# Selective-scan kernel: the products with B issued behind the first scan of an index, and both products of the next chunk's first two indices inside the last index

## The chip, the cores and the metric

The kernel runs on one core of a Trainium2 chip. The metric is the device time of one execution in microseconds, the median of the runs. Engines are named as in the profile: PE is TensorE, DVE is VectorE, ACT is ScalarE, POOL is GpSimd, SP is SyncE (here it only issues DMAs).

## The reference

The whole program is a block of three layers over x with shape (4, 2048, 256): half of an attention and mixture-of-experts layer, a bidirectional selective scan (Mamba) layer, and again half of the first. Only the selective scan is touched. Cut down, for one direction, with 512 inner channels d and 16 states n:

```python
x  = silu(depthwise_conv4(x) + conv_b)                   # (B, 512, L)
dt, Bm, Cm = split(x_proj_w @ x)                          # 16 + 16 + 16 rows
dt = softplus(dt_w @ dt + dt_b)
def step(h, (dt_t, B_t, C_t, u_t)):                       # over the L tokens
    h = exp(dt_t * A) * h + (dt_t * u_t) * B_t            # h is (B, 512, 16)
    return h, sum_n h * C_t
y = scan(step) + D * x
```

The other direction runs over the reversed tokens, and the two results are added.

## The kernel before

The scan stage is `mamba_scans`. The 4 x 2048 tokens are cut into chunks of 512 (`CH`), 16 chunks for each direction, so the stage handles M = 32 chunks one after the other. The 512 channels are four tiles m of 128 partitions (`DM` = 4). A chunk has 16 indices n (`DS`), one for each state; a pair (n, m) is a unit, and a chunk has 64 units in the order n outer, m inner. `par` is the chunk's parity.

For one index n the work is this:

- **Decay** (ACT, L1911): exp(dt * A) of a unit into one of two PSUM banks. The decay of unit k waits until the scan of unit k - 2 is done.
- **Product with B** for the whole index, 128 x 2048. For 11 of the 16 indices DVE computes it (`times_b` of the vector block, L1969): `du` times a row of B that PE has spread over a PSUM bank (`BANK_B`) with four transposes (`row_b`, L1752). The two buffers `db` alternate. For n in `POOL_N` = (3, 6, 9, 12, 15) POOL computes it from an SBUF row (L1688) into the single buffer `dbp`, three indices ahead: POOL issues the one for n + 3 behind its own work for n.
- **Scan** (DVE, L1998): `tensor_tensor_scan`, one for each unit, 128 x 512, reads the decay, the product and the carried state, and writes `h[n % 4]`.
- **Carry** (ACT, L1871): the last column of `h` is kept for the next chunk. It is issued at the second unit of the next index, when all four scans of index n are done.
- **Times C** (POOL, L1695): `h[n % 4]` times a row of C, 128 x 2048, when the carry is done. POOL's order in a chunk is: times C of 0; product 3; times C of 1, 2, 3; product 6; times C of 4, 5, 6; product 9; times C of 7, 8, 9; product 12; a DMA that adds up softplus; times C of 10, 11; `du` of the next chunk (L1682); times C of 12; product 15; times C of 13, 14, 15.
- **Sum** (PE, L1779): four fp32 matmuls by the identity (eight passes in the trace) add `h * C` up in PSUM. PE does it two indices late (`LAG`). The scan of index n waits (`summed`) for the sum of index n - 4, since `h` has four buffers.

Into the same indices the next chunks' preparation is spread by constants. PE: projection of x at index 0, turning of B at 2, dt projections at 3 to 6, convolution of the chunk after the next at 7 to 14, two halves for each m (`PE_CONV`), and `add_other` at 9 in the second direction. ACT, at the second unit (m = 1): `split` at index 1, `keep_b` at 3, `softplus_in` at 4 to 7, `conv_out` (L1835) at 9, 11, 13 and 15, and `silu` (L1839, L1840: table load, 128 x 2048 activation, table load back) at 15; and at all four units: `read_y` at 2, `softplus_exp` at 8, `softplus_ln` at 9.

PE's row for a DVE product follows the product before: `next_row_b(i, par, n)` stands in PE's index n - 1, waits until DVE has made the product of n, and spreads the row of the next DVE index.

The engines run in the order in which they are written; nothing is reordered. The chunk loop `in_steps` writes 12 of the 32 chunks out (chunks 0 to 3 and 12 to 19) and runs the other 20 in two hardware loops of four chunks for each pass (2 passes over chunks 4 to 11, 3 over chunks 20 to 31). In the loops the semaphore values are computed in registers.

The vector block's order before is, for each index n: at m = 0, if n + 1 (modulo 16) is a DVE index, a wait until every scan issued so far is done (`scanned`), then the product of n + 1, then the four scans of n. So the product of index 0 of the next chunk stands ahead of the scans of index 15, and that of index 1 ahead of the scans of index 0.

Of the kernel before, what the change touches and what calls it, by code (L numbers as in the profile page):

```python
# [20 lines left out]
DI, DS, DTR = 512, 16, 16  # L21
DM = DI // P
# [3 lines left out]
UNITS = DM * DS  # L26
# [4 lines left out]
class Phase:  # L31
# [12 lines left out]
    def sem(self, name):  # L44
        self.sems.append(self.nc.alloc_semaphore(f"{self.tag}_{name}"))
        return self.sems[-1]
# [1456 lines left out]
def mamba_scans(nc, tag, psum, ident, xp, y, both, weights, B, S):  # L1503
# [9 lines left out]
    POOL_N = (3, 6, 9, 12, 15)  # L1513
# [5 lines left out]
    BANK_A, BANK_B, BANK_X = 4, 6, 7  # L1519
    FREE = (BANK_A, BANK_A + 1, BANK_X, 0)  # L1520
    PE_X, PE_TURN, PE_DT, PE_CONV, PE_Y, SP_Y = 0, 2, 3, 7, 9, 11
    A_SPLIT, A_TURN, A_SOFT, A_EXP, A_LN, A_SILU = 1, 3, 4, 8, 9, 15
    G_ADD, G_DU = 9, 11
    EXP_LN = "natural_log_exp_and_others"

    def b_count(i, n):

        made = POOL_N if n in POOL_N else DVE_N
        return len(made) * i + sum(z <= n for z in made)
# [6 lines left out]
    with Phase(nc, tag) as ph:  # L1536
# [34 lines left out]
        scanned, carried, hc_ready, summed = sem("scanned"), sem("carried"), sem("hc_ready"), sem("summed")  # L1571
# [25 lines left out]
        def chunk_of(i, par, n):  # L1597

            return (i, par, n) if n < DS else (i + 1, 1 - par, n - DS)

        with nc.Block() as block:
# [226 lines left out]
            def _(act):  # L1828
# [13 lines left out]
                def split(i):  # L1842
                    act.wait_ge(xp_ps, i + 1)
                    act.wait_ge(bc_out, 16 * i)
                    nc.scalar.activation(xd[:, :], psum[0:BC + DTR, BANK_X, :], ACT.Copy).then_inc(xd_sb, 1)
# [15 lines left out]
                def softplus_exp(i, m):  # L1861
                    act.wait_ge(dt_read, 2 * (DM * i + m + 1))
                    nc.scalar.activation(sp1[:, m, :], sp1[:, m, :], ACT.Exp, scale=-1.0).then_inc(exps, 1)

                def softplus_ln(i, m):
                    act.wait_ge(exps, DM * i + m + 1)
                    nc.scalar.activation(sp1[:, m, :], sp1[:, m, :], ACT.Ln, bias=1.0).then_inc(logs, 1)

                def carry(n, ends, rev):
                    kept = zeros[:, :] if ends else h[n % NH][:, :, LAST[rev]]  # L1870
                    nc.scalar.activation(state[:, n, :], kept, ACT.Copy).then_inc(carried, 1)  # L1871

                def read_y(i, m):
                    act.wait_ge(y_done, DM * i + m + 1)
                    if m == 0:
                        act.wait_ge(stored, 16 * i)
                    nc.scalar.activation(yo[:, m, :], psum[:, m, :], ACT.Copy).then_inc(y_read, 1)
# [22 lines left out]
                def step(i, par, first, opens, ends, way):  # L1900
                    for k, (n, m) in enumerate(UNIT):
                        if k >= 2 or not first:
                            act.wait_ge(scanned, UNITS * i + k - 1)
                        if k == 0 and first:
                            act.wait_ge(dt_ready, 1)
                        elif k == 0:
                            act.wait_ge(dt_added, 16 * i)
                        if m == 1 and (n or not first):
                            act.wait_ge(scanned, UNITS * i + DM * n)
                            carry((n - 1) % DS, ends if n else opens, way(0 if n else -1))  # L1910
                        nc.scalar.activation(psum[:, BANK_A + k % 2, :], dt[par][:, m, :], ACT.Exp, scale=an[way(0)][:, m, n:n + 1]  # L1911
                                             ).then_inc(decay, 1)
                        if n == LAG and not first:
                            read_y(i - 1, m)
                        if n == A_EXP:
                            softplus_exp(i + 1, m)
                        if n == A_LN:
                            softplus_ln(i + 1, m)
                        if m != 1:
                            continue  # L1920
                        if n == A_SPLIT:
                            split(i + 1)
                        if n == A_TURN:
                            keep_b(i + 1, 1 - par)
                        if A_SOFT <= n < A_SOFT + DM:
                            softplus_in(i + 1, 1 - par, n - A_SOFT, way(1))
                        if n > PE_CONV and (n - PE_CONV) % 2 == 0:
                            conv_out(i + 2, par, (n - PE_CONV) // 2 - 1, way(2))
                        if n == A_SILU:
                            silu(i + 2, par)  # L1930
# [6 lines left out]
            @block.vector  # L1937
            def _(dve):
                nc.vector.memset(state[:, :, :], 0.0).then_inc(cleared, 1)
                nc.vector.memset(zeros[:, :], 0.0).then_inc(cleared, 1)  # L1940
                def diagonals(d):
                    for m in range(DM):
                        for j in range(TAPS):
                            ins = nc.vector.tensor_scalar(cwd[d][:, m, j, :], ident[:, :], cw[d][:, m, j:j + 1], None, ALU.mult)
                    ins.then_inc(diags, 1)

                def skips(d):
                    for m in range(DM):
                        ins = nc.vector.tensor_scalar(dwd[d][:, m, :], ident[:, :], dw[d][:, m:m + 1], None, ALU.mult)
                    ins.then_inc(diags, 1)  # L1950

                def negate(d):
                    dve.wait_ge(a_exp, d + 1)
                    nc.vector.tensor_scalar(an[d][:, :, :], an[d][:, :, :], -1.0, None, ALU.mult).then_inc(a_neg, 1)
                dve.wait_ge(cw_in, 16)
                diagonals(0)
                dve.wait_ge(w_in[0], 96)
                skips(0)
                negate(0)
                dve.wait_ge(w_in[1], 112)  # L1960
                diagonals(1)
                skips(1)
                dve.wait_ge(cleared, 2)

                def times_b(i, par, n):
                    dve.wait_ge(b_ps, b_count(i, n))
                    if n == 0:
                        dve.wait_ge(du_ready, i + 1)
                    nc.vector.tensor_tensor(db[b_turn(par, n)][:, :, :], du[par][:, :, :],  # L1969
                                            psum[:, BANK_B, :].unsqueeze(1).to_broadcast([P, DM, CH]), ALU.mult).then_inc(dve_b, 1)  # L1970

                dve.wait_ge(logs, DM)
                nc.vector.tensor_tensor(dt[0][:, :, :], sp1[:, :, :], dt[0][:, :, :], ALU.add).then_inc(dt_ready, 1)
                dve.wait_ge(dt_ready, 1)
                nc.vector.tensor_tensor(du[0][:, :, :], dt[0][:, :, :], u[0][:, :, :], ALU.mult).then_inc(du_ready, 1)
                times_b(0, 0, 0)
                negate(1)

                def step(i, par, first, opens, ends, way):
                    for k, (n, m) in enumerate(UNIT):  # L1980
                        if m == 0:
                            if (n + 1) % DS not in POOL_N:
                                if k or not first:
                                    dve.wait_ge(scanned, UNITS * i + k)
                                times_b(*chunk_of(i, par, n + 1))
                            if not first:
                                dve.wait_ge(carried, DS * (i - 1) + n + 1)
                            if n == NH - 1 and not first:
                                dve.wait_ge(y_done, DM * i)
                            elif n >= NH:  # L1990
                                dve.wait_ge(summed, (DS - 1) * i + n - NH + 1)
                            elif not first:
                                dve.wait_ge(summed, (DS - 1) * (i - 1) + n + DS - NH + 1)
                            dve.wait_ge(pool_b if n in POOL_N else dve_b, b_count(i, n))
                        made_b = dbp if n in POOL_N else db[b_turn(par, n)]
                        dve.wait_ge(decay, UNITS * i + k + 1)
                        flip = FLIP[way(0)]
                        nc.vector.tensor_tensor_scan(h[n % NH][:, m, flip], psum[:, BANK_A + k % 2, flip], made_b[:, m, flip],  # L1998
                                                     state[:, n, m:m + 1], ALU.mult, ALU.add).then_inc(scanned, 1)
                in_steps(dve, step)  # L2000


# [346 lines left out]
```

## Time and profile before

| what | value |
|---|---|
| median of 3 runs | 8392.39 us (8386.71 to 8393.45) |
| profiled execution, its own time | 8391.64 us |
| its span | 8389.9 us |
| PE busy | 7633.5 us (91%) |
| DVE busy | 7255.9 us (86%) |
| ACT busy | 5015.7 us (60%) |
| POOL busy | 3693.2 us (44%) |

The shares are means over stages that are limited by different engines; the scan stage lies between 2612 and 5959 us of the span. A duration of an instruction in the timeline is longer than what it adds when it follows another of its engine, since the end of one overlaps the start of the next; the difference of two starts is what it adds.

### The profile page before, as it was taken

The numbers are of one execution on the slowest core, as the hardware profiler recorded it, in microseconds if no ns is written. First come the engines' busy times: TensorE is split into PE (matmuls) and PEld (weight loads), VectorE is DVE, ScalarE is ACT, GpSimd is POOL, SyncE is SP. The second block draws the span as 40 slices with busy tenths as digits, with TensorE's granted clock in tenths as the row PEclk, the third lists the DMA queues.
The fourth block names the chain that finished last, engine by engine and source line by source line (L and its number), as shares of the span: only waits on it lengthen the run. The fifth ranks groups of instructions, "written<-read, shape, count | busy, mean of one in ns | idle before, by whom it ended". The sixth has DMA issues, their size and how long they took to land. (4 is left out here: it accounts for less than half of the span.)

```text
span 8389.9 us, 132293 instructions
## 1 busy us (share of the span) xinstructions
PE 7633.5 (91%) x40012; PEld 3197.5 (38%) x40012; DVE 7255.9 (86%) x10619; ACT 5015.7 (60%) x7151; POOL 3693.2 (44%) x1326
## 2 busy tenths in 40 slices
PE   6999999989988888888889999898889999999899
PEld 3333333325543333333333333333553333333355
DVE  6988888858877999999999999999658888888588
ACT  3577777773255666566666666666316777777622
POOL 0010000110015999999999999999510001101000
PEclk9899999999999999999999999999988999999999
DMA  6101101112263222222233333333670001010121
GB/s 178 18 19 20 20 19 20 19 33 68 73 205 115 86 84 84 84 84 84 84 95 94 96 95 92 95 93 95 203 223 16 19 20 20 20 27 13 37 80 60
DMA packets 532315, 605.82 MB, mean 72 GB/s; under 512 B 195520, under 2 KB 344768, under 8 KB 527616
## 3 DMA queue, kind: packets, MB, share of 16 engines
q1 hardware_dynamic: 527104, 564.73, 22.8%
q0 software_dynamic: 4608, 33.56, 2.0%
q8 instruction: 317, 5.19, 0.3%
q14 instruction: 286, 2.34, 0.1%
HBM read 399.85 MB, written 163.69 MB: 67 GB/s over the span
## 5 line engine op out<-in xcount | busy, mean ns | idle before, releaser
L833 DVE TENSOR_REDUCE ffn_att_mx<-psum 128x1 f32<-128x512 f32 (+3 forms) x4608 | 2725.7, 652 | 357.2 <-PE psum L674 204.1
L794 ACT ACTIVATE ffn_att_e<-psum,unscale 128x1024 f32<-128x1024 f32 (+3 forms) x2560 | 2376.8, 985 | 756.5 <-PE psum L739 750.5
L1695 POOL TENSOR_TENSOR scan_h<-scan_h,scan_cs 128x2048 f32<-128x2048 f32 x512 | 2334.8, 4626 | 228.1 <-ACT scan_state L1871 228.1
L1779 PE MATMUL psum<-scan_h,ident 128*128 128x512 f32 x4096 | 1961.5, 624 | 108.1 <-POOL scan_h L1695 108.0
L1998 DVE TENSOR_TENSOR_SCAN scan_h<-psum,scan_state,scan_db 128x512 f32<-128x512 f32 x1408 | 1677.4, 1261 | 10.6 <-ACT psum L1911 10.6
L641 POOL TENSOR_SCALAR_AFFINE_SELECT ffn_att_e<-ffn_att_e 128x512 f32<-128x512 f32 x512 | 324.6, 634 | 3012.3 <-ACT ffn_att_e L794 3012.3
L674 PE MATMUL psum<-ffn_att_k,ffn_att_q 48*128 48x512 f16 (+3 forms) x5120 | 1435.6, 367 | 174.7 <-DMA ffn_att_v<-v 59.2
L705 PE MATMUL psum<-ffn_att_e,ffn_att_v 128*32 128x512 f32 (+3 forms) x10240 | 1238.1, 556 | 8.1 <-ACT ffn_att_o L809 2.6
L1779 PEld LDWEIGHTS psum<-scan_h,ident 128*128 128x128 f32 x4096 | 795.6, 199 | 1176.6 <-issue 1038.5
L1911 ACT ACTIVATE psum<-scan_dt,scan_anr 128x512 f32<-128x512 f32 x1024 | 700.0, 686 | 542.5 <-DVE scan_h L1998 542.2
L1911 ACT ACTIVATE psum<-scan_dt,scan_anf 128x512 f32<-128x512 f32 x1024 | 699.8, 686 | 534.5 <-DVE scan_h L1998 533.9
L674 PEld LDWEIGHTS psum<-ffn_att_k,ffn_att_q 48*128 48x128 f16 x5120 | 395.0, 94 | 1564.0 <-DVE ffn_att_mx L833 1260.6
L739 PE MATMUL psum<-ffn_att_q,ffn_att_k 50*128 50x512 f16 (+3 forms) x5120 | 811.7, 355 | 56.2 <-ACT ffn_att_e L794 24.9
L1969 DVE TENSOR_TENSOR scan_db<-scan_du,psum 128x2048 f32<-128x2048 f32 x353 | 807.3, 2287 | 40.7 <-issue 6.1
L1998 DVE TENSOR_TENSOR_SCAN scan_h<-psum,scan_state,scan_dbp 128x512 f32<-128x512 f32 x640 | 771.7, 1264 | 61.3 <-ACT psum L1911 60.3
L1688 POOL TENSOR_TENSOR scan_dbp<-scan_du,scan_bs 128x2048 f32<-128x2048 f32 x160 | 732.8, 4580 | 0.0
L1180 DVE SCALAR_TENSOR_TENSOR ffn_out_acc<-psum,ffn_out_comb,ffn_out_acc 128x256 f32<-128x256 f32 x896 | 433.3, 484 | 64.3 <-PE psum L1045 28.7
L678 PE MATMUL psum<-ffn_att_mask,ffn_att_pick 64*128 64x128 bf16 x4096 | 435.4, 221 | 0.0
L983 POOL TENSOR_TENSOR ffn_out_ul<-ffn_out_uT,ffn_out_uh 128x1024 f16<-128x1024 f32 x32 | 68.1, 2129 | 808.4 <-ACT ffn_out_uh L1094 808.4
L1752 PE MATMUL psum<-ident,scan_bt 128*128 128x128 f32 x1416 | 224.5, 281 | 200.5 <-DVE scan_db L1969 199.4
L1045 PE MATMUL psum<-ffn_out_eh,ffn_out_uh 128*128 128x512 f16 x1024 | 389.5, 380 | 1.5 <-DVE ffn_out_acc L1180 1.5
L1045 PE MATMUL psum<-ffn_out_el,ffn_out_uh 128*128 128x512 f16 x1024 | 389.5, 380 | 0.0
(252 smaller groups left out, 7319.9 us busy)
## 6 DMA issues: line engine op xcount, KB each, us to landing
scan_cs<-scan_bcd SPq DMA_DIRECT2D x520, 256.0 KB, 3.1
scan_bs<-scan_bcd SPq DMA_DIRECT2D x162, 256.0 KB, 3.4
scan_win<-xp SPq DMA_DIRECT2D x34, 1036.0 KB, 7.0
scan_dt<-scan_sp POOLq DMA_DIRECT2D x32, 1024.0 KB, 6.9
mamba_out_ffn_in_ys<-both SPq DMA_DIRECT2D x18, 1024.0 KB, 7.7
mamba_out_ffn_in_zt<-zs SPq DMA_DIRECT2D x18, 1024.0 KB, 10.6
scan_yi<-y SPq DMA_DIRECT2D x17, 1024.0 KB, 6.7
ffn_att_q<-q_parts SPq DMA_DIRECT2D x128, 128.0 KB, 2.9
```

The source lines that it names most:

```text
L674: ins = nc.tensor.matmul(psum[:, turn, j * w:(j + 1) * w], q[at, i // HALF, pair, i % HALF * P:(i % HALF + 1) * P], k[at, c * P:c * P + w] ...
L705: ins = nc.tensor.matmul(psum[32 * h:32 * h + VW, BANK_O, off:CH], V[par][:, kb, :], E[:, s % PB, h, off:CH], start=kb == 0, stop=closes(s ...
L739: ins = nc.tensor.matmul(psum[:, h, off:CH], k[at, kb * P:(kb + 1) * P], q[at, qb * CH // (HALF * P), h // 2, qb * CH % (HALF * P) + off:q ...
L794: nc.scalar.activation(E[:, s % PB, 2 * hp:2 * hp + 2, off:CH], psum[:, 2 * hp:2 * hp + 2, off:CH], ACT.Exp, scale=unscale[:, 0:1]).then_i ...
L833: nc.vector.reduce_max(mx[:, hh * 2 + pairs[0]:hh * 2 + pairs[1], i // HALF, i % HALF, c // TT], psum[:, turn, 0:(pairs[1] - pairs[0]) * w ...
L1045: ins = nc.tensor.matmul(psum[:, BANKS_E[n % 4], :], u[:, k, t * P:(t + 1) * P], w[:, k, 2 * e:2 * e + 2, :], start=k == 0 and p == 0, sto ...
L1688: nc.gpsimd.tensor_tensor(dbp[:, :, :], du[par][:, :, :], bs[turn][:, :].unsqueeze(1).to_broadcast([P, DM, CH]), ALU.mult).then_inc(pool_b, 1)
L1695: nc.gpsimd.tensor_tensor(h[n % NH][:, :, :], h[n % NH][:, :, :], cs[:, n % NCS, :].unsqueeze(1).to_broadcast([P, DM, CH]), ALU.mult).then ...
L1779: ins = nc.tensor.matmul(psum[:, m, :], ident[:, :], h[n % NH][:, m, :], start=False, stop=n == DS - 1)
L1911: nc.scalar.activation(psum[:, BANK_A + k % 2, :], dt[par][:, m, :], ACT.Exp, scale=an[way(0)][:, m, n:n + 1]).then_inc(decay, 1)
L1969: nc.vector.tensor_tensor(db[b_turn(par, n)][:, :, :], du[par][:, :, :], psum[:, BANK_B, :].unsqueeze(1).to_broadcast([P, DM, CH]), ALU.mu ...
L1998: nc.vector.tensor_tensor_scan(h[n % NH][:, m, flip], psum[:, BANK_A + k % 2, flip], made_b[:, m, flip], state[:, n, m:m + 1], ALU.mult, A ...
```

## The change

The product of index n + 1 is issued at m = 1, that is behind the first scan of index n and ahead of the second. It still waits until the scans of index n - 1 are done. In index 0 none is issued. In index 15 (whose own product is POOL's) two are issued: that of the next chunk's index 0 at m = 1, and that of its index 1 at m = 2, ahead of the third scan. The prologue makes the product of index 1 of the first chunk, so the first chunk's order is as before. In the last chunk both products are made too, for a chunk that doesn't exist. On ACT the last `conv_out` of a chunk moves from the second unit of index 15, where it stood behind that unit's decay, to behind the first unit's decay. PE, POOL and SP keep their order.

```diff
-    A_SPLIT, A_TURN, A_SOFT, A_EXP, A_LN, A_SILU = 1, 3, 4, 8, 9, 15
+    A_SPLIT, A_TURN, A_SOFT, A_EXP, A_LN, A_LAST, A_SILU = 1, 3, 4, 8, 9, 15, 15
 ...
                         if n == LAG and not first:
                             read_y(i - 1, m)
+                        if m == 0 and n == A_LAST:
+                            conv_out(i + 2, par, DM - 1, way(2))
 ...
-                        if n > PE_CONV and (n - PE_CONV) % 2 == 0:
+                        if PE_CONV < n < A_LAST and (n - PE_CONV) % 2 == 0:
                             conv_out(i + 2, par, (n - PE_CONV) // 2 - 1, way(2))
 ...
                 times_b(0, 0, 0)
                 negate(1)
+                times_b(0, 0, 1)
 
                 def step(i, par, first, opens, ends, way):
                     for k, (n, m) in enumerate(UNIT):
+                        if m == 1 and (n + 1) % DS not in POOL_N and n:
+                            dve.wait_ge(scanned, UNITS * i + DM * n)
+                            times_b(*chunk_of(i, par, n + 1))
+                        if m == 2 and n == DS - 1:
+                            times_b(i + 1, 1 - par, 1)
                         if m == 0:
-                            if (n + 1) % DS not in POOL_N:
-                                if k or not first:
-                                    dve.wait_ge(scanned, UNITS * i + k)
-                                times_b(*chunk_of(i, par, n + 1))
                             if not first:
                                 dve.wait_ge(carried, DS * (i - 1) + n + 1)
```

## Rows read from the trace of the kernel before

**Rows 1.** The page: its span, and its groups of the scan stage.

```profile
span 8389.9 us, 132293 instructions
...
L1695 POOL TENSOR_TENSOR scan_h<-scan_h,scan_cs 128x2048 f32<-128x2048 f32 x512 | 2334.8, 4626 | 228.1 <-ACT scan_state L1871 228.1
...
L1998 DVE TENSOR_TENSOR_SCAN scan_h<-psum,scan_state,scan_db 128x512 f32<-128x512 f32 x1408 | 1677.4, 1261 | 10.6 <-ACT psum L1911 10.6
...
L1969 DVE TENSOR_TENSOR scan_db<-scan_du,psum 128x2048 f32<-128x2048 f32 x353 | 807.3, 2287 | 40.7 <-issue 6.1
L1998 DVE TENSOR_TENSOR_SCAN scan_h<-psum,scan_state,scan_dbp 128x512 f32<-128x512 f32 x640 | 771.7, 1264 | 61.3 <-ACT psum L1911 60.3
```

**Rows 2.** Busy time of the engines: stage, one loop chunk, one written-out chunk.

```profile
core 0: us, PE busy (x) PEld busy (x) DVE busy (x) ACT busy (x) POOL busy (x), PEclk, DMA share, GB/s
2612.50:5949.00 3336.50, 2980.94 (x7532) 1265.56 (x7533) 3224.04 (x2400) 2028.00 (x3481) 3182.72 (x735) 0.96 0.30 89
...
4477.19:4580.76 103.57, 94.90 (x241) 40.96 (x242) 100.88 (x75) 63.47 (x110) 99.77 (x24) 0.95 0.32 95
```

**Rows 3.** Timeline of DVE, a written-out chunk, from one scan (15, 0) to the next.

```profile
start us, us, engine line op out<-in xcount [idle before <-releaser]
...
4474.79 2.29 DVE L1969 TENSOR_TENSOR scan_db<-scan_du,psum 128x2048 f32<-128x2048 f32 x1
4477.19 2.46 DVE L1998 TENSOR_TENSOR_SCAN scan_h<-psum,scan_state,scan_dbp 128x512 f32<-128x512 f32 x2
4481.51 2.46 DVE L1998 TENSOR_TENSOR_SCAN scan_h<-psum,scan_state,scan_dbp 128x512 f32<-128x512 f32 x2 [1.86 <-ACT psum L1911]
4484.00 2.29 DVE L1969 TENSOR_TENSOR scan_db<-scan_du,psum 128x2048 f32<-128x2048 f32 x1
4486.20 4.80 DVE L1998 TENSOR_TENSOR_SCAN scan_h<-psum,scan_state,scan_db 128x512 f32<-128x512 f32 x4
4491.04 2.29 DVE L1969 TENSOR_TENSOR scan_db<-scan_du,psum 128x2048 f32<-128x2048 f32 x1
4493.24 9.50 DVE L1998 TENSOR_TENSOR_SCAN scan_h<-psum,scan_state,scan_db 128x512 f32<-128x512 f32 x8
...
4512.02 7.15 DVE L1998 TENSOR_TENSOR_SCAN scan_h<-psum,scan_state,scan_db 128x512 f32<-128x512 f32 x6
4519.51 2.46 DVE L1998 TENSOR_TENSOR_SCAN scan_h<-psum,scan_state,scan_db 128x512 f32<-128x512 f32 x2 [0.33 <-ACT psum L1911]
...
4542.99 4.80 DVE L1998 TENSOR_TENSOR_SCAN scan_h<-psum,scan_state,scan_dbp 128x512 f32<-128x512 f32 x4
...
4568.81 9.50 DVE L1998 TENSOR_TENSOR_SCAN scan_h<-psum,scan_state,scan_db 128x512 f32<-128x512 f32 x8
4578.35 2.29 DVE L1969 TENSOR_TENSOR scan_db<-scan_du,psum 128x2048 f32<-128x2048 f32 x1
4580.76 2.46 DVE L1998 TENSOR_TENSOR_SCAN scan_h<-psum,scan_state,scan_dbp 128x512 f32<-128x512 f32 x2
4585.06 2.46 DVE L1998 TENSOR_TENSOR_SCAN scan_h<-psum,scan_state,scan_dbp 128x512 f32<-128x512 f32 x2 [1.84 <-ACT psum L1911]
```

**Rows 4.** Timeline of POOL in the same chunk: times C of 1 and 2, 9, product 15.

```profile
4500.44 9.01 POOL L1695 TENSOR_TENSOR scan_h<-scan_h,scan_cs 128x2048 f32<-128x2048 f32 x2
...
4548.24 4.54 POOL L1695 TENSOR_TENSOR scan_h<-scan_h,scan_cs 128x2048 f32<-128x2048 f32 x1 [0.74 <-ACT scan_state L1871]
...
4575.76 4.80 POOL L1688 TENSOR_TENSOR scan_dbp<-scan_du,scan_bs 128x2048 f32<-128x2048 f32 x1
```

**Rows 5.** Timeline of DVE, a chunk of the first hardware loop.

```profile
3331.38 2.45 DVE L1998 TENSOR_TENSOR_SCAN scan_h<-psum,scan_state,scan_dbp 128x512 f32<-128x512 f32 x2
...
3385.98 9.50 DVE L1998 TENSOR_TENSOR_SCAN scan_h<-psum,scan_state,scan_db 128x512 f32<-128x512 f32 x8
3395.60 2.29 DVE L1969 TENSOR_TENSOR scan_db<-scan_du,psum 128x2048 f32<-128x2048 f32 x1
3397.81 4.80 DVE L1998 TENSOR_TENSOR_SCAN scan_h<-psum,scan_state,scan_dbp 128x512 f32<-128x512 f32 x4
...
3435.82 2.45 DVE L1998 TENSOR_TENSOR_SCAN scan_h<-psum,scan_state,scan_dbp 128x512 f32<-128x512 f32 x2
```

**Rows 6.** Timeline of POOL in that loop chunk.

```profile
3402.99 4.53 POOL L1695 TENSOR_TENSOR scan_h<-scan_h,scan_cs 128x2048 f32<-128x2048 f32 x1 [0.96 <-ACT scan_state L1871]
...
3430.48 4.78 POOL L1688 TENSOR_TENSOR scan_dbp<-scan_du,scan_bs 128x2048 f32<-128x2048 f32 x1
```

**Rows 7.** Timeline of ACT in index 15 of the written-out chunk.

```profile
4584.34 1.30 ACT L1911 ACTIVATE psum<-scan_dt,scan_anr 128x512 f32<-128x512 f32 x2
```

**Rows 8.** Timeline of PE, indices 9, 10, 14 and 15 of the written-out chunk.

```profile
4543.13 0.65 PE L1752 MATMUL psum<-ident,scan_bt 128*128 128x128 f32 x4 [0.79 <-DVE scan_db L1969]
...
4554.36 3.60 PE L1779 MATMUL psum<-scan_h,ident 128*128 128x512 f32 x8
...
4576.31 3.60 PE L1779 MATMUL psum<-scan_h,ident 128*128 128x512 f32 x8
4580.69 0.65 PE L1752 MATMUL psum<-ident,scan_bt 128*128 128x128 f32 x4 [0.79 <-DVE scan_db L1969]
4585.08 5.26 PE L1779 MATMUL psum<-scan_h,ident 128*128 128x512 f32 x8 [3.73 <-POOL scan_h L1695]
```

## Prediction

> **What bounds the kernel.** I read the page first [rows 1]. The change touches one stage only, so the chain that ended last (it lies in the last stage) says nothing about it; I turned to the busy time of the engines within the scan stage [rows 2]. There DVE is busy for 3224.0 of 3336.5 us (97%) and POOL for 3182.7 (95%), PE for 2980.9 and ACT for 2028.0. Two engines are nearly full, so the question for each microsecond that DVE gives up is whether POOL lets it. DVE's idle time on the page is 60.3 and 10.6 us of scans waiting for ACT's decays and 40.7 us ahead of the products; none is put down to POOL.
>
> The timeline of DVE [rows 3] shows a written-out chunk. I count from the start of the first scan of index 15, called S, to the next S: 4477.19 to 4580.76, 103.57 us. In a hardware loop the same distance is 3331.38 to 3435.82, 104.44 us [rows 5]. Each chunk falls into two stretches, cut at the end of the last scan of index 9, called E.
>
> - **S to E.** Written out: E is 4542.99 + 4.80 = 4547.79, so 70.60 us. In the loop: 3397.81 + 4.80 = 3402.61, so 71.23 us. DVE sets this stretch: POOL waits in it for carries, also ahead of times C of 9 [rows 4, 6].
> - **E to S.** Written out 32.97, in the loop 33.21. POOL starts times C of 9 0.45 us after E (4548.24), then works without a gap to the end of product 15 (4575.76 + 4.80 = 4580.56), which is 32.32 us [rows 4]. Scan (15, 0) reads that product and starts 0.20 later, at 4580.76. The same 0.20 stands at 4477.19. DVE alone would have been there 0.21 us earlier: the product ahead starts at 4578.35, and a scan starts 2.20 after the start of a product. So written out, POOL already sets this stretch, and no time can be won in it. In the loop POOL needs 3402.99 - 3402.61 = 0.38, then 3430.48 + 4.78 - 3402.99 = 32.27, then 0.20: 32.85 of 33.21 [rows 6]. There 0.36 us can be won.
>
> **The change part by part.** Prices from [rows 3]: eight scans in a row take 9.50, one 1.26, so a scan adds 1.178. A product adds 2.20 ahead of the scan behind it (4491.04 to 4493.24).
>
> *The wait ahead of the product.* Today the product starts when the last scan has ended. From the start of that scan it is 1.297 us (4486.20 + 3 x 1.178 = 4489.73, to 4491.04 is 1.30), against 1.178 where a scan follows a scan: the wait costs 0.12 us. In the loop it is 3385.98 + 7 x 1.178 = 3394.23 to 3395.60, 1.37: 0.20 us [rows 5]. In the new order the scans waited for ended an instruction ago. No row shows a product behind an unfinished scan. Its bounds are 1.178 and 1.30 (1.37 in the loop). I take 1.178: the pair in the other order, product then scan, overlaps by 0.09 and scan then scan by 0.08, so the kind of the two does not seem to matter.
>
> The Trainium skill states the opposite for this engine: in "VectorE: DVE Perf Modes", section "The DRAIN you can't avoid", chained operations and operations with a semaphore after each took the same time, so the wait costs nothing. Our rows, with 0.12 and 0.20 us for it, do not agree; by that rule the saving of this part would be zero, and the time that of the first rival below.
>
> *The stall of index 15.* Scans three and four of index 15 start 4.32 us after S instead of 2.36 (4481.51): a stall of 1.97 us. ACT sets it: from the end of scan (14, 3), 4568.81 + 9.50 = 4578.31, ACT needs until 4584.34 for carry, decay, conv_out, table load, silu, table load [rows 7], and then 0.72 until the scan at 4585.06. In the new order conv_out (about 0.6) is out of this chain, so the third scan may start about 6.1 us after the end of scan (14, 3). DVE gets there later: scan, product, scan, product take 2 x 1.178 + 2 x 2.20 = 6.76 after S, and S is itself held by product 15. The stall is gone, 1.97 us, with room over.
>
> *The product that changes stretch.* The product of the next index 0 moves from ahead of S to behind it, 2.20 us. Ahead of S it stood where POOL sets the time, so nothing is won there: DVE alone would need from E 20 scans and three products, about 23.6 + 6.6 = 30.1 us, POOL 32.97, and DVE now stands 2.8 us idle for product 15, with the two products queued behind the scan that waits. So the cover of this product, the wait for POOL, is lost, and its 2.20 us land in the stretch that DVE sets. The product of index 1 stays in S to E, as do 2, 4, 5, 7, 8 and 10: eight products in place of seven.
>
> *Sum for S to E.* Written out: stall -1.97, seven waits of 0.12 -0.84, one product +2.20: -0.61, giving 69.99. In the loop: -1.97, seven waits of 0.20 -1.40, +2.20: -1.17, giving 70.06. E to S: 0 written out, -0.36 in the loop. The stall of 0.33 in index 5 stays: no product stands in index 5, before or after.
>
> *Does POOL or PE take it back?* POOL does 22 operations a chunk, 16 times C, 5 products and `du`, each 4.48 start to start (9.01 - 4.53 in [rows 4]), about 99.2 with 0.6 for the DMA's issue, against a new period of 103. Its waits for carries shift: times C of 15 now waits for scan (15, 3), which ends 9.2 us after S, and starts at 9.65 instead of 8.7; times C of 0 follows at 14.3, product 3 is ready at 23.5, scan (3, 0) wants it at 25.5. The same sum for products 6, 9 and 12 leaves about 2 us each. PE: row 1 of the next chunk must be spread between the two products of index 15. The first ends 3.47 after S; PE answers 0.05 later and takes 0.65 [rows 8], so it is there at 4.2; the second product wants it at 4.55. PE is free by then: its sum before that row ends at 4579.9, and waits 0.79 us for the product. The tightest place is scan (12, 0), which waits for the sum of index 8: that sum ends at 4557.96, 10.2 after E [rows 8]; PE's work from index 9 on follows the product of 10, for which PE waits [rows 8], and which comes 1.2 us later against E, so 11.4, and scan (12, 0) wants it at 11.5. Being late there costs nothing below 2.8 us, the slack ahead of S. So all these edits cost zero; without that cover a late sum would cost its own length in each chunk.
>
> *Ends.* The first chunk has six waits and no stall in front of it: -0.7. At the very end two products stand ahead of scan (15, 2), so times C of 15 starts about 1.5 us later: +1.5. The jump at the loop heads, put down as issue ahead of the products (6.1 us) [rows 1], stays.
>
> **Sum.** Written-out stretches S to E: 11 x -0.61 = -6.7. Loop chunks: 20 x -(1.17 + 0.36) = -30.6. Ends +0.8. Together -36.5 us. Against the profiled execution's 8391.64 this is 8355.1; the median of the runs is 0.75 above it, so I predict 8355.5 us, 0.44% below the median. About 0.2% (17 us) is what a measurement of this kernel can tell from no change.
>
> **Rivals.**
> 1. *The wait was free to remove but the drain stays*: a product behind a scan still starts 1.30 after it. Then S to E has eight times 0.12 more: 31 x 0.96 + 0.7 = +30, so 8386, no change. With the loop's 0.20 kept too: 20 x 1.6 + 11 x 0.96 + 0.7 = +43, so 8399, no change as well. Chance 0.14 for both. For it: no row shows the pair. Against it: the overlap of 0.08 and 0.09 in both pairs that are shown.
> 2. *The row for the second product is late* (slower). If PE took up that row only behind the sum of index 13, which starts 4.3 us after S and takes 5.26 [rows 8], the second product would start at about 10.2 instead of 4.55: 32 x 5.6 = 180 us, so 8535. It decides from 1.7 us of lateness in a chunk on: (36.5 + 17) / 32. Against it: the row stands ahead of that sum in PE's order, and PE waits 0.79 us at that place now. Chance 0.05.
> 3. *Part of the saving is taken back by late sums*: PE's sums or ACT's decays hold scans of indices 0 to 9 for about 0.5 us a chunk, most at indices 8 and 9, where ACT works without a gap: 8371. For it: PE is at 92% of the chunk [rows 2]. Against it: 2 us of slack at each sum I followed. Chance 0.14.
> 4. *More is won*: POOL is less tight than I think, the stretch E to S shrinks. It would take a shorter POOL chain of seven operations, which nothing shortens. 8335 at most. Chance 0.03.
>
> **How the numbers follow.** The forecast (8345 to 8366) has 0.64. Faster by over 0.2% means below 8375.6: the forecast, rival 3 mostly and rival 4, 0.80. Within 0.2%: rival 1 and the rest of 3, 0.15. Slower: rival 2, 0.05. The range 8342 to 8386 takes in rival 3 and the static form of rival 1 and leaves out the others.
>
> **What will show it.** In the new timeline of DVE: product starts 1.18 after the scan ahead of it (1.30 if rival 1 holds); S to E 70.0 written out and 70.1 in the loop; E to S 32.97 and 32.85, with an idle time of about 2.8 us ahead of scan (15, 0) that ends when product 15 does; no idle time ahead of scan (15, 2); scans waiting for ACT 60 us before, about 11 after. In PE's timeline row 1 ends before 4.55 us after S. The prediction is wrong if the second product of index 15 waits for PE, if the idle time ahead of scan (15, 0) is much over 3 us, or if a scan in indices 0 to 9 waits for a sum.

## The result, and the profile after

The change takes the median from 8392.92 us (4 runs) to 8344.17 us (8340.5 to 8344.98, 4 runs): -48.8 us, ratio 0.9938 with a 95% interval of [0.9923, 0.9953]. The direction was forecast and the mechanism holds, but the sum was too small: -36.5 us forecast, 12 short. The measured median lies 2 us above the lower end of the range (8342); the ratio, applied to the 8392.39 us that the forecast started from, gives 8340, 2 us below it.

The page after: the span, and the groups that answer to [rows 1].

```profile
span 8338.8 us, 132262 instructions
...
L1695 POOL TENSOR_TENSOR scan_h<-scan_h,scan_cs 128x2048 f32<-128x2048 f32 x512 | 2338.4, 4617 | 175.7 <-ACT scan_state L1871 175.5
...
L2002 DVE TENSOR_TENSOR_SCAN scan_h<-psum,scan_state,scan_db 128x512 f32<-128x512 f32 x1408 | 1690.8, 1265 | 12.5 <-ACT psum L1911 12.2
...
L2002 DVE TENSOR_TENSOR_SCAN scan_h<-psum,scan_state,scan_dbp 128x512 f32<-128x512 f32 x640 | 786.4, 1268 | 84.5 <-POOL scan_dbp L1688 59.2
...
L1971 DVE TENSOR_TENSOR scan_db<-scan_du,psum 128x2048 f32<-128x2048 f32 x354 | 801.9, 2265 | 0.3
```

The scan is now line 2002, the product 1971. The 60.3 us for ACT ahead of the `dbp` scans are gone. In their place stand 84.5 us, the wait forecast ahead of scan (15, 0). The page puts 59.2 of them down to POOL's product; those that it puts down to PE are POOL's too, as the timeline below shows. The idle time ahead of the products falls from 40.7 to 0.3 us, and their mean from 2287 to 2265 ns.

Busy time of the engines in the stage, from the start of its first scan to the end of its last, the answer to [rows 2]:

```profile
2612.80:5900.50 3287.70, 2993.31 (x7535) 1275.98 (x7536) 3190.58 (x2401) 2010.15 (x3481) 3186.84 (x735) 0.96 0.30 90
```

The stage took 3336.5 us before and 3287.7 after: -48.8. The executions differ outside it too: in those of this study the span less this stage was between 5029 and 5059 us, though nothing was changed there. So the stage's own time is the sharper measure, and I give it for each experiment. It comes from one profiled execution of each kernel; two executions of the changed kernel gave 3287.7 and 3287.6.

The timeline of DVE after, a written-out chunk, the answer to [rows 3] (columns as there):

```profile
4350.00 1.28 DVE L2002 TENSOR_TENSOR_SCAN scan_h<-psum,scan_state,scan_dbp 128x512 f32<-128x512 f32 x1 [2.70 <-POOL scan_dbp L1688]
4351.20 2.26 DVE L1971 TENSOR_TENSOR scan_db<-scan_du,psum 128x2048 f32<-128x2048 f32 x1
4353.38 1.28 DVE L2002 TENSOR_TENSOR_SCAN scan_h<-psum,scan_state,scan_dbp 128x512 f32<-128x512 f32 x1
4354.67 2.29 DVE L1971 TENSOR_TENSOR scan_db<-scan_du,psum 128x2048 f32<-128x2048 f32 x1
4356.87 2.45 DVE L2002 TENSOR_TENSOR_SCAN scan_h<-psum,scan_state,scan_dbp 128x512 f32<-128x512 f32 x2
...
4382.43 1.26 DVE L2002 TENSOR_TENSOR_SCAN scan_h<-psum,scan_state,scan_db 128x512 f32<-128x512 f32 x1
4383.61 2.27 DVE L1971 TENSOR_TENSOR scan_db<-scan_du,psum 128x2048 f32<-128x2048 f32 x1
4385.79 5.98 DVE L2002 TENSOR_TENSOR_SCAN scan_h<-psum,scan_state,scan_db 128x512 f32<-128x512 f32 x5
4392.10 2.46 DVE L2002 TENSOR_TENSOR_SCAN scan_h<-psum,scan_state,scan_db 128x512 f32<-128x512 f32 x2 [0.33 <-ACT psum L1911]
...
4416.32 3.63 DVE L2002 TENSOR_TENSOR_SCAN scan_h<-psum,scan_state,scan_dbp 128x512 f32<-128x512 f32 x3
...
4452.92 1.28 DVE L2002 TENSOR_TENSOR_SCAN scan_h<-psum,scan_state,scan_dbp 128x512 f32<-128x512 f32 x1 [2.77 <-PE psum L1779]
```

S is 4350.00, E is 4416.32 + 3.63 = 4419.95, the next S 4452.92: 69.95 and 32.97. Forecast were 69.99 and 32.97. Over the written-out chunks the means are 69.88 and 32.92. A product starts 1.18 us after the scan ahead of it (4382.43 to 4383.61) and adds 2.18, not 2.20 (4383.61 to 4385.79). Scan (15, 2) waits for nothing. Ahead of scan (15, 0) DVE stands 2.70 and 2.77 us idle. The second wait is put down to PE: the scan waits for product 15 and for the sum of index 11. POOL's and PE's timelines there:

```profile
4447.89 4.83 POOL L1688 TENSOR_TENSOR scan_dbp<-scan_du,scan_bs 128x2048 f32<-128x2048 f32 x1
```

```profile
4444.17 3.59 PE L1779 MATMUL psum<-scan_h,ident 128*128 128x512 f32 x8
4447.60 1.88 PE L1713 MATMUL psum<-scan_win,scan_cwdr 128*128 128x512 f32 x4
4449.32 3.59 PE L1779 MATMUL psum<-scan_h,ident 128*128 128x512 f32 x8
```

The sum of index 11 is the first of the two and ended at 4447.76, 5.16 us before the scan. PE is named only because the next sum, that of index 12, for which this scan doesn't wait, happened to end at 4452.91. POOL's product ended at 4452.72, and the scan starts 0.20 behind it, as it does where POOL is named. So POOL sets this start too. In all 31 chunks the sum of index 11 had ended at least 4.2 us before the scan.

### The profile page after: what moved, and what is told of

Same layout as the page of the kernel before. It is cut to its first block and busy times, and to the rows that moved or that the text cites. A ratio compares the mean times of both kernels' runs of the same rounds, so it can differ in the third digit from the quotient of the medians.

```text
span 8338.8 us, 132262 instructions
## 1 busy us (share of the span) xinstructions
PE 7642.3 (92%) x40011; PEld 3210.4 (39%) x40012; DVE 7225.0 (87%) x10620; ACT 4998.1 (60%) x7151; POOL 3695.7 (44%) x1326
## 5 line engine op out<-in xcount | busy, mean ns | idle before, releaser
L2002 DVE TENSOR_TENSOR_SCAN scan_h<-psum,scan_state,scan_dbp 128x512 f32<-128x512 f32 x640 | 786.4, 1268 | 84.5 <-POOL scan_dbp L1688 59.2
L739 PE MATMUL psum<-ffn_att_q,ffn_att_k 50*128 50x512 f16 (+3 forms) x5120 | 807.6, 354 | 56.2 <-ACT ffn_att_e L794 25.7
L1971 DVE TENSOR_TENSOR scan_db<-scan_du,psum 128x2048 f32<-128x2048 f32 x354 | 801.9, 2265 | 0.3
```

The source lines that it names most:

```text
L739: ins = nc.tensor.matmul(psum[:, h, off:CH], k[at, kb * P:(kb + 1) * P], q[at, qb * CH // (HALF * P), h // 2, qb * CH % (HALF * P) + off:q ...
```

## The experiments

Two sets of four kernels ran, each with runs of the kernel before on the same chip; the medians of these are 8385.92 us (experiments 1, 3, 4 and 6) and 8389.05 us (2, 5 and 7). The theory of the prediction is A: POOL sets E to S, DVE sets S to E, so what counts is how many products stand in DVE's stretch, what each costs with its wait, and what is stalled there.

**1. The wait back, in the new order.** Each product waits for every scan issued.

```diff
                         if m == 1 and (n + 1) % DS not in POOL_N and n:
-                            dve.wait_ge(scanned, UNITS * i + DM * n)
+                            dve.wait_ge(scanned, UNITS * i + k)
 ...
                         if m == 2 and n == DS - 1:
+                            dve.wait_ge(scanned, UNITS * i + k)
                             times_b(i + 1, 1 - par, 1)
```

> The changed kernel, but each product waits for all scans issued before it. Theory A (that wait costs 0.12 us written out, 0.20 in a loop, of a product in DVE's stretch): 11 x 0.96 + 20 x 1.6 + 1 = +43 us, 8387. Theory C (the wait is free, as the Trainium skill's page says of chained operations; the gain came from the stall of index 15): 8344, no change against the changed kernel.

Measured: 8388.35 us, ratio 1.0007 [0.9997, 1.0016]; the stage 3340.4 us, +52.6 against the changed kernel. The whole gain is gone with one semaphore value. Timeline of DVE in this kernel, index 4 of a written-out chunk:

```profile
4359.37 1.26 DVE L2003 TENSOR_TENSOR_SCAN scan_h<-psum,scan_state,scan_db 128x512 f32<-128x512 f32 x1
4360.66 2.29 DVE L1971 TENSOR_TENSOR scan_db<-scan_du,psum 128x2048 f32<-128x2048 f32 x1
4362.87 8.33 DVE L2003 TENSOR_TENSOR_SCAN scan_h<-psum,scan_state,scan_db 128x512 f32<-128x512 f32 x7
```

The product starts 1.29 after the scan in place of 1.18, and adds 2.21 in place of 2.18. Both parts belong to the wait. Theory C falls: the wait costs 0.14 us a product written out, and in the loops about 0.25 in the mean, since S to E grew there from 69.87 to 71.84 with eight products.

**2. The new place of index 15's product alone**, everything else as before the change, every wait on all scans:

```diff
+                        if m == 1 and n == DS - 1:
+                            dve.wait_ge(scanned, UNITS * i + k)
+                            times_b(i + 1, 1 - par, 0)
                         if m == 0:
-                            if (n + 1) % DS not in POOL_N:
+                            if n < DS - 1 and n + 1 not in POOL_N:
```

> The kernel before with one edit: the product of the next index 0 stands behind scan (15, 0) in place of ahead of it; every wait stays on all scans issued. Theory A: the stall of 1.97 us is gone, but the product, 2.2 us and 0.12 to 0.20 for its wait, lands in DVE's stretch: +0.35 in 11 written-out chunks, and in 20 loop chunks +0.43 less the 0.42 that POOL's stretch gets shorter: +4 us, no change against the kernel before. Theory B (the stall is the gain): 31 x -1.97 = -60 us, -0.7%.

Measured: 8394.55 us, ratio 1.0006 [0.9996, 1.0015]; the stage 3342.4, +5.9 against before (expected +4). The waits of DVE on other engines in it:

```profile
DVE scan_h L2001 <- POOL scan_dbp L1688: 66.5, 31, 2.4
DVE scan_h L2001 <- ACT psum L1911: 10.0, 30, 0.3
DVE scan_db L1969 <- issue: 5.8, 3, 2.0
```

The stall of index 15 is gone from the list, ACT's 60 us have become POOL's 66, and no time was won. This is the part of the change that looks best in the profile of before.

**3. The other half alone**: products behind the first scan with the weaker wait in indices 0 to 14, index 15 and conv_out as before the change. Against the changed kernel this puts the product of index 1 into index 0, behind its first scan. The diff, against the changed kernel (for conv_out it is that of experiment 5):

```diff
-                times_b(0, 0, 1)
 ...
-                        if m == 1 and (n + 1) % DS not in POOL_N and n:
-                            dve.wait_ge(scanned, UNITS * i + DM * n)
+                        if m == 1 and n < DS - 1 and n + 1 not in POOL_N:
+                            if n or not first:
+                                dve.wait_ge(scanned, UNITS * i + DM * n)
                             times_b(*chunk_of(i, par, n + 1))
-                        if m == 2 and n == DS - 1:
-                            times_b(i + 1, 1 - par, 1)
+                        if m == 0 and n == DS - 1:
+                            dve.wait_ge(scanned, UNITS * i + k)
+                            times_b(i + 1, 1 - par, 0)
```

> Only half of the change: products behind the first scan with the weaker wait in indices 0 to 14; index 15 as in the kernel before, with one product ahead of its first scan behind all scans, and conv_out at its second unit. Theory A: the stall of 1.97 us stays and the product of 2.2 us is back under POOL's cover; seven waits are saved (-0.84 written out, -1.4 in a loop), POOL's stretch is 0.36 shorter in a loop: 11 x -0.84 - 20 x 1.76 = -44, 8348: nearly the whole gain. Theory B or C (the gain is the stall of index 15): 8385 to 8393.

Measured: 8330.74 us, ratio 0.9933 [0.9916, 0.9949]; the stage 3280.3, 56.2 under before and 7.4 under the changed kernel. Theory A stands and was even too low by 12. One part is the product's own 0.02 us. The other is that the stall shrinks: POOL holds scan (15, 0) back while ACT's silu goes on (written out it starts 2.80 us after the product ahead of it, before the change 2.36), so of the stall's 1.97 us about 1.6 are left written out and 1.75 in the loops. Against this, the three periods with a loop's jump became only 0.9 us shorter each where 1.76 was expected. Set beside the changed kernel, this run says that what the change moves into index 15 cost 7.4 us of the stage, too little for the medians to tell (ratios 0.9933 and 0.9938).

**4. One product in index 15 in place of two.**

```diff
-                times_b(0, 0, 1)
 ...
-                        if m == 1 and (n + 1) % DS not in POOL_N and n:
-                            dve.wait_ge(scanned, UNITS * i + DM * n)
+                        if m == 1 and (n + 1) % DS not in POOL_N:
+                            if n or not first:
+                                dve.wait_ge(scanned, UNITS * i + DM * n)
                             times_b(*chunk_of(i, par, n + 1))
-                        if m == 2 and n == DS - 1:
-                            times_b(i + 1, 1 - par, 1)
```

> Products stand behind the first scan of every index, index 0 included, so index 15 holds only the product of the next index 0; the rest is as in the changed kernel. Theory A (POOL sets the stretch from the last scan of index 9 to the first of index 15, DVE the rest, so a product costs 2.2 us wherever it stands in DVE's stretch): still eight products there, ACT is ready 3.3 us after scan (15, 0) and scan (15, 2) wants it at 4.5, so no stall; the only loss is the jump of the hardware loop, which is again uncovered by queued work, about 2 us at 3 loop heads: 8350 us, +6 against the changed kernel. Theory B (it takes both products in index 15 to hide the silu): the stall of 1.97 us is back in each chunk, 8405.

Measured: 8345.89 us, ratio 0.9954 [0.994, 0.9967]; the stage 3296.4, +8.7 against the changed kernel. The periods are those of the changed kernel (102.75 written out, 102.60 in the loops) but for the three that cross a loop's jump: 106.3 against 102.95, 10 us together. Theory B falls. What the second product in index 15 buys is cover for the jump: the branch from the end of a hardware loop's body back to its start. Timeline of DVE at the first jump, changed kernel first:

```profile
3428.59 1.28 DVE L2002 TENSOR_TENSOR_SCAN scan_h<-psum,scan_state,scan_dbp 128x512 f32<-128x512 f32 x1
3429.88 2.29 DVE L1971 TENSOR_TENSOR scan_db<-scan_du,psum 128x2048 f32<-128x2048 f32 x1
3432.08 2.45 DVE L2002 TENSOR_TENSOR_SCAN scan_h<-psum,scan_state,scan_dbp 128x512 f32<-128x512 f32 x2
3434.68 5.99 DVE L2002 TENSOR_TENSOR_SCAN scan_h<-psum,scan_state,scan_db 128x512 f32<-128x512 f32 x5
```

and the kernel with one product:

```profile
3415.24 3.63 DVE L2000 TENSOR_TENSOR_SCAN scan_h<-psum,scan_state,scan_dbp 128x512 f32<-128x512 f32 x3
3421.40 1.28 DVE L2000 TENSOR_TENSOR_SCAN scan_h<-psum,scan_state,scan_db 128x512 f32<-128x512 f32 x1 [2.53 <-ACT scan_state L1871]
```

In the one the next chunk starts 0.15 us after the last scan's end, in the other 2.53. (The carry that this scan waits for had long been done.) In both the next chunk's first DVE instruction starts at nearly the same distance from S, 9.47 and 9.54 us. ACT comes late from the same jump. Its decay for that scan, in the kernel with one product:

```profile
3420.36 0.69 ACT L1911 ACTIVATE psum<-scan_dt,scan_anf 128x512 f32<-128x512 f32 x1 [3.12 <-issue]
```

It starts 8.50 us after S, where in a loop chunk without a jump it starts 5.87 after S, and it ends 0.35 us before the scan starts. At the three jumps of this kernel DVE stands 2.26 to 2.55 us idle in this way. The rest of the 3.7 us by which such a period is longer in the mean are mostly waits for ACT's decays in the 27 us after S, 0.47 to 1.81 us together.

**5. The last conv_out back at the second unit**, all else as in the changed kernel:

```diff
-                        if m == 0 and n == A_LAST:
-                            conv_out(i + 2, par, DM - 1, way(2))
 ...
-                        if PE_CONV < n < A_LAST and (n - PE_CONV) % 2 == 0:
+                        if PE_CONV < n and (n - PE_CONV) % 2 == 0:
```

> The changed kernel with the last conv_out back at the second unit of index 15. Theory A: ACT is ready for scan (15, 2) 4.0 us after scan (15, 0) in place of 3.3, and DVE wants it at 6.8: no change against the changed kernel. Theory E (moving conv_out is what frees the scans): 0.6 us in each chunk, +19 us.

Measured: 8336.27 us, ratio 0.9942 [0.9929, 0.9956]; the stage 3288.4. The changed kernel beside it gave 8335.0, ratio 0.9938 [0.9925, 0.9952], and a stage of 3287.6. The move of conv_out is worth nothing here.

What was expected of that second measurement of the changed kernel:

> The changed kernel once more, on the chip of the other runs, as their measure. Both theories: the ratio to the kernel before as first measured, 0.992 to 0.995.

**6. The product of index 0 ahead of scan (15, 0)**, where DVE idles for POOL, and that of index 1 behind it:

```diff
-                        if m == 1 and (n + 1) % DS not in POOL_N and n:
+                        if m == 1 and (n == DS - 1 or n and n + 1 not in POOL_N):
                             dve.wait_ge(scanned, UNITS * i + DM * n)
-                            times_b(*chunk_of(i, par, n + 1))
-                        if m == 2 and n == DS - 1:
-                            times_b(i + 1, 1 - par, 1)
+                            times_b(*(chunk_of(i, par, n + 1) if n < DS - 1 else (i + 1, 1 - par, 1)))
+                        if m == 0 and n == DS - 1:
+                            dve.wait_ge(scanned, UNITS * i + DM * (n - 1))
+                            times_b(i + 1, 1 - par, 0)
```

> The product of the next index 0 stands ahead of scan (15, 0), waiting only for the scans of index 13, where DVE otherwise idles 2.7 us for POOL's product 15; the product of the next index 1 stands behind scan (15, 0); the rest is as in the changed kernel. Theory A: DVE's stretch loses a product of 2.2 us in 31 chunks, POOL's stretch stays 32.9 (DVE needs 32.3 of it): -68 us, and up to +6 at the loop heads: 8276 to 8282. Theory D (POOL, busy for 99.2 us a chunk, or PE with its sums, takes over): the period stays over 102, 8330 to 8344.

Measured: 8306.72 us, ratio 0.9913 [0.9893, 0.9932]; the stage 3248.7, 39 under the changed kernel where 62 to 68 were expected, so theory A's mechanism is there and its size is not. E to S stayed at 32.94 written out with the product in it: that stretch is POOL's. But the periods go between 100.6, as theory A has it, and 102.3. The time is lost in index 2. The three views of one such place, DVE first, then ACT, then PE:

```profile
4342.80 5.12 DVE L2003 TENSOR_TENSOR_SCAN scan_h<-psum,scan_state,scan_db 128x512 f32<-128x512 f32 x4
4349.19 1.28 DVE L2003 TENSOR_TENSOR_SCAN scan_h<-psum,scan_state,scan_db 128x512 f32<-128x512 f32 x1 [1.26 <-ACT psum L1911]
```

```profile
4347.88 0.60 ACT L1877 ACTIVATE scan_yo<-psum 128x512 f32<-128x512 f32 x1 [1.72 <-PE psum L1779]
4348.38 0.20 ACT L1871 ACTIVATE scan_state<-scan_h 128x4 f32<-128x4 f32 x1
4348.47 0.68 ACT L1911 ACTIVATE psum<-scan_dt,scan_anr 128x512 f32<-128x512 f32 x1
```

```profile
4332.16 6.76 PE L1779 MATMUL psum<-scan_h,ident 128*128 128x512 f32 x8 [3.85 <-POOL scan_h L1695]
...
4346.82 3.60 PE L1779 MATMUL psum<-scan_h,ident 128*128 128x512 f32 x8
```

PE idles 3.85 us for POOL, then its sum of index 13 takes 6.76 us where a sum elsewhere takes 3.60: the granted clock in 4332.1 to 4338.7 was 0.53 of 2.4 GHz, that is nearly all of it at 1.2 GHz. PE works without a gap from there, and the chunk's last sum starts at 4346.82. ACT's `read_y` waits 1.72 us for it, the carry and the decay of (2, 1) are queued behind `read_y`, and DVE waits 1.26 us for that decay. Which periods are long follows the sum of index 13: away from the jumps it took 5.1 to 5.4 us in all 15 periods of 100.5 to 101.0 us, and 6.3 to 6.8 in all 13 of 101.8 to 102.3, behind the same 3.8 to 4.1 us of idle time.

**7. The same, with read_y one unit later**, so that a decay is always ahead of it:

```diff
-                        if n == LAG and not first:
-                            read_y(i - 1, m)
+                        if LAG * DM < k <= LAG * DM + DM and not first:
+                            read_y(i - 1, k - LAG * DM - 1)
```

> As the run with the next index 0's product ahead of scan (15, 0), and ACT reads the four sums y of the chunk before one unit later, behind the decays of (2, 1), (2, 2), (2, 3) and (3, 0). Theory F (in that run the period goes between 100.6 and 102.2 us because ACT waits for PE's last sum at index 2 with the decays queued behind it): the period is 100.6 to 100.8 nearly everywhere, 31 x -0.8 = -25 us against that run, 1.15 to 1.2% under the kernel before. Theory G (PE itself is too late, whoever waits for it): the wait goes to a scan that wants a sum, and the time stays.

Measured: 8277.2 us, ratio 0.9865 [0.985, 0.988]; the stage 3228.1, 20.6 under the run before and 108.4 under the kernel before. 25 us against that run were expected. The periods are 100.4 to 101.1 but for the three with a jump, 103.0, and this although the sum of index 13 still took 6.2 to 6.8 us in 14 of 31 chunks. Theory F stands, G falls. This version beats both kernels. POOL's groups between 2650 and 5850 us, ahead of which it now idles 41.9 us in all:

```profile
L1695 POOL TENSOR_TENSOR scan_h<-scan_h,scan_cs 128x2048 f32<-128x2048 f32 x507 | 2322.4, 4699 | 41.9 <-ACT scan_state L1871 41.9
...
L1688 POOL TENSOR_TENSOR scan_dbp<-scan_du,scan_bs 128x2048 f32<-128x2048 f32 x158 | 736.1, 4659 | 0.0
```

## Why the prediction was right in its mechanism and short in its sum

- **Right: POOL sets E to S.** 32.97 forecast, 32.92 measured written out; 32.85 and 32.78 in the loops, where scan (15, 0) starts 0.12 behind POOL's product and not 0.20. A product put into that stretch costs nothing (experiment 6); one taken out of it wins nothing written out and 0.43 us in a loop, where 0.36 was forecast (experiment 2).
- **Right: the stall goes and the moved product eats it.** Experiment 2 shows the two as a wash, +5.9 us for the stage.
- **Right: the wait ahead of a product is what is won.** Experiment 1 takes it back and the gain is zero. The value that I chose for the unseen pair, 1.178, is what the trace shows. The Trainium skill's statement in "VectorE: DVE Perf Modes", "The DRAIN you can't avoid", that a semaphore between two operations costs nothing extra does not hold for this pair: 1.18 without the wait and 1.29 with it.
- **Wrong in size: a product's 2.20.** That figure was read from products which had waited. Without the wait a product adds 2.18, so the wait is worth 0.14 and not 0.12 written out, and in the loops 0.23 to 0.25 and not 0.20. S to E came out at 69.88 written out (69.99 forecast, and the step from [rows 3] was 70.60 where the mean of before is 70.68) and 69.87 in the loops (70.06). By means of before and after: 11 x -0.79 = -8.7 where -6.7 stood, and for 17 loop periods 102.66 - 104.50 = -1.84 where -1.53 stood. That is 7.3 us, of which the 0.07 less in E to S of the loops is about 1.
- **Wrong: "the jump at the loop heads stays".** Before, the three periods with a jump took 1.86 us more than their neighbours, after 0.29. They got 3.40 us shorter each where 1.53 stood: 5.6 us. I priced the jump as a fixed stall behind DVE's work. The runs show a start that hardly moves against S, 8.6 to 9.7 us after it wherever DVE stood idle for it, and work that DVE has queued up to there covers it: DVE's idle time was 1.83 to 2.19 us at the jumps before and 0 to 0.38 after.
- Against these 12.9 us stands the tail behind the last S, which is 2.4 us longer and not 1.5. With that the 12 us are accounted for. One slip is in the sum itself: 8355.1 and 0.75 give 8355.9, not 8355.5.
- **Rival 2, the late row, was nearer than I said.** The row was expected in 0.65 us and to be there at 4.2, and in 16 of 31 chunks it was. In 12 it took 1.1 us, in 3 something between. PE's timeline after, in one of these:

```profile
4353.52 1.12 PE L1752 MATMUL psum<-ident,scan_bt 128*128 128x128 f32 x4 [3.46 <-DVE scan_db L1971]
```

The granted clock of the stretch from 4353.50 to 4354.60 was 0.50, 1.2 GHz, after 3.46 us in which PE had nothing to do; before the change it idled 0.79 there and had the full clock. The row ends at 4354.64, the product starts at 4354.67, 0.11 late. A small price, but in these chunks the cover that I counted on was gone.
- **Rival 3, late sums, did not occur** in the changed kernel at any size that matters, and is what limits the next step: it took back about 0.7 us a chunk in experiment 6.

What stays open: why the wait costs more in a loop than written out. The registers that carry the loop's semaphore values are at hand as a cause; no run isolated them. Open too is what sets the start behind a jump, and which share of it is ACT's. In experiment 3 that decay was there 6.2 us after S and DVE still started 8.9 to 9.35 after S, so there DVE's own jump set it; at the second jump of the changed kernel and the third of experiment 7 the scan started 0.03 and 0.06 us behind ACT's decay, so there ACT's did.

## What to carry to other kernels

Cut a period at the points where the engine that sets it changes, and price an edit in its own stretch: an instruction moved from under another engine's cover costs its full length, and a stall that an idle neighbour would have covered is worth little. A wait for the last instruction of the same engine cost 0.14 to 0.25 us each here; wait for the one that the data needs. If a reader of a late result shares a queue with work that others wait for, put it behind that work.

## What the runs showed of the hardware

- **A wait on the scan just issued costs DVE 0.14 us** written out (1.29 + 2.21 against 1.18 + 2.18), and about 0.25 in a hardware loop, by S to E of experiment 1.
- **Behind a hardware loop's jump an engine starts late, and work that it has queued covers the delay.** DVE's first instruction behind the jump started 8.6 to 9.0 us after S before the change, 9.2 to 9.6 after it, 9.3 to 9.6 in experiment 4 and 8.9 to 9.35 in experiment 3. DVE's idle time was 0 to 0.38 us in the changed kernel, where its work reached to 9.2 or 9.3 us after S, and 2.26 to 2.55 in experiment 4, where it ended at 7.0. From the end of the last decay to that start it was between 3.4 us (experiment 2) and 4.7 us (experiment 3) where DVE stood idle, so this is no constant. The Trainium skill, "Runtime: NRT & Kernel Launch", section "Instruction fetch mechanics", says that a taken branch to code outside the window held breaks the prefetch and waits for a fetch. That fits; no run here shows the fetch itself.
- **PE's clock after a short idle.** Behind 3.46 and 3.85 us without work the next stretch ran at 0.50 and 0.53 of 2.4 GHz: four transposes took 1.12 us in place of 0.65, a sum 6.76 in place of 3.60. The length of the idle time alone doesn't tell it: behind 3.58 us without work the same four transposes took 0.65 in another chunk of the changed kernel (at 3942.31), and the sum behind them 5.40.
